# A hybrid layer on one core: group 0 of the mixer taken out of its loop and mixed with the making of the decay tables, and one PSUM bank with fewer early users

## The reference, cut to what matters

```python
zxbcdt = hidden_states @ in_proj_w.T          # gate, x, B, C and dt
xBC = silu(causal_conv4(xBC) + conv_b)
dt = softplus(dt + dt_bias);  A = -exp(A_log) # 128 heads
A_cumsum = cumsum(A * dt)                     # per head, over the tokens
Y_diag = (C B^T * exp(segment_sum)) @ (x*dt)  # inside a chunk
states = ...                                  # from chunk to chunk, decayed
y = (Y_diag + Y_off + D*x) * silu(gate)
out = rmsnorm_per_group(y) @ out_proj_w.T     # 8 groups of 16 heads
```

## Time and profile before

| | us |
|---|---|
| median of 3 runs | 2069.37 (2069.25 to 2069.98) |
| the profiled execution | 2066.19 |
| its span | 2064.4 |
| PE busy | 1975.3 (96%) |
| DVE busy | 1497.6 (73%) |
| ACT busy | 1182.6 (57%) |
| POOL busy | 1033.3 (50%) |
| start of c0 in groups 0, 1 and 2 | 63.27, 263.56, 461.31 |

### The profile page before, as it was taken

How to read it: one execution, slowest core, us unless ns; L and a number is a source line. 1 busy time by engine, 2 the same in 40 slices (tenths; PEclk the granted TensorE clock), 3 DMA queues, 4 the chain that set the end, 5 groups by cost and what they waited for, 6 DMA issues and landing times.

```text
span 2064.4 us, 39384 instructions
## 1 busy us (share of the span) xinstructions
PE 1975.3 (96%) x11776; PEld 1637.7 (79%) x11776; DVE 1497.6 (73%) x2825; ACT 1182.6 (57%) x2569; POOL 1033.3 (50%) x907
## 2 busy tenths in 40 slices
PE   3899999999999999999999999999999999998998
PEld 2688878888888888888888887888788777776876
DVE  6698589859985997699669867985898571186215
ACT  3596369637953784387449645963696325432441
POOL 1288139714960595179318922881497125240433
PEclk7899999999999999999999999999999999999999
DMA  2443035203521451235134313430352049931995
GB/s 86 136 142 103 27 105 163 78 31 116 167 67 38 125 158 51 70 109 145 42 89 124 111 42 94 147 99 27 105 166 75 23 163 387 362 111 42 364 397 182
DMA packets 143909, 261.75 MB, mean 127 GB/s; under 512 B 19536, under 2 KB 35920, under 8 KB 143696
## 3 DMA queue, kind: packets, MB, share of 16 engines
q1 hardware_dynamic: 134848, 231.35, 35.3%
q0 software_dynamic: 7520, 24.65, 3.6%
q10 hardware_dynamic: 1328, 3.15, 0.4%
HBM read 233.38 MB, written 25.69 MB: 125 GB/s over the span
## 4 chain that ended last, share of the span: by engine, by line
PE 65%; issue 20%; DVE 6%; POOL 6%; ACT 1%; DMA 1%; another core or an unknown queue 0%; DVEq 0%; POOLq 0%; SPq 0%; ACTq 0%
PE bank L1602 35%; PE bank L1737 6%; PE bank L1751 5%; PE bank L1892 5%; POOL Y L728 4%; PE bank L1692 4%; PE bank L1904 3%; PE bank L1720 2%; DVE Y L1244 1%; PE bank L1879 1%; PE bank L1711 1%; PE bank L1610 1%; DVE quad L1167 1%; DVE Y L1253 1%; DVE X L1488 1%
## 5 line engine op out<-in xcount | busy, mean ns | idle before, releaser
L1602 PE MATMUL bank<-xh,wh 128*128 128x512 f32 x1288 | 524.3, 407 | 17.1 <-POOL wl L711 13.1
L1602 PE MATMUL bank<-xh,wl 128*128 128x512 f32 x1288 | 505.5, 392 | 0.0
L1602 PE MATMUL bank<-xl,wh 128*128 128x512 f32 x1288 | 502.9, 390 | 0.0
L711 POOL TENSOR_TENSOR wl<-raw,wh 128x512 fp32r<-128x512 f32 x144 | 192.3, 1340 | 486.8 <-ACT wh L886 486.8
L1244 DVE SCALAR_TENSOR_TENSOR Y<-bank,cpar,Y 128x511 f32<-128x511 f32 (+2 forms) x384 | 286.9, 747 | 22.9 <-ACT Y L932 13.8
L1602 PEld LDWEIGHTS bank<-xh,wh 128*128 128x128 f32 x1288 | 243.4, 189 | 65.2 <-issue 18.0
L1602 PEld LDWEIGHTS bank<-xh,wl 128*128 128x128 f32 x1288 | 242.5, 188 | 54.6
L1602 PEld LDWEIGHTS bank<-xl,wh 128*128 128x128 f32 x1288 | 243.8, 189 | 46.1 <-issue 0.5
L728 POOL TENSOR_TENSOR Y<-Y,gt 128x512 f32<-128x512 f32 x128 | 185.8, 1451 | 94.4 <-DVE gt L1298 92.7
L1306 DVE TENSOR_TENSOR al<-Y,ah 128x512 fp32r<-128x512 f32 x128 | 95.7, 747 | 169.1 <-ACT ah L990 169.1
L1602 PE MATMUL bank<-wh,ah 128*128 128x512 f32 x544 | 213.7, 393 | 2.4 <-DVE X L1514 1.7
(11 more groups left out here) (229 smaller groups left out, 4066.0 us busy)
## 6 DMA issues: line engine op xcount, KB each, us to landing
mem<-c_rows SPq DMA_DIRECT2D x128, 256.0 KB, 3.8
mem<-wffn_d SPq DMA_DIRECT2D x62, 512.0 KB
E<-e_rows SPq DMA_DIRECT2D x256, 96.0 KB, 3.3
raw<-wconv_d SPq DMA_DIRECT2D x80, 256.0 KB, 2.7
cv<-c_rows SPq DMA_DIRECT2D x64, 256.0 KB, 3.9
spare<-c_rows SPq DMA_DIRECT2D x64, 256.0 KB, 4.3
raw<-wgate_d SPq DMA_DIRECT2D x64, 256.0 KB, 2.7
raw<-wout_d SPq DMA_DIRECT2D x64, 256.0 KB, 2.7
```

The costliest lines, as they stand in the source:

```text
L711: inc(pool.tensor_tensor(wl[:, W_SLOT[p], :], raw[:, R_SLOT[p], :], wh[:, W_SLOT[p], :], ALU.subtract), w_lo)
L1602: got = mm(out, l, r, start=first and n == 0, stop=last and n == 2)
```

## The change: what it does

1. **Group 0 leaves the loop.** The body of the loop becomes a function `tick(i, k)` on each engine. `tick(0, k)` is written out for all k, then `Fori(1, GROUPS)` runs the rest. The barrier `PH_PREP` is gone.
2. **Preparation is mixed in.** PE does c0, c1 and c2 right after the dt projection, and then the transposes and last-sum products. ACT starts tick 0 after the exponentials of v, makes the row tables after tick 0 and the head tables after tick 3. DVE does its whole polynomial and scan first, then tick 0, the sum table, ticks 1 and 2, the subtraction, tick 3 and so on.
3. **The polynomial is halved.** v, |v|, exp and all polynomial steps run per batch of 512 tokens instead of over 1024. PREP's event numbers grow from 13 to 24 for dt, and so on.
4. **Buffers move** so that the tables and the first tiles don't overlap: tables into the upper half of `Y`, sums into `cv`, dt into `gt`, dt weights into `quad` and slot 10 of `wh`/`wl`. SP no longer waits before the first weights. In group 0 SP asks for the head tables at tick 5 instead of 2, and all row loads come behind that.
5. **Banks.** In groups 1 to 7 the early list is one shorter, and the state bank has one early user. In group 0 all big tiles rotate over banks 0, 1, 2, since the special ones hold preparation data.

```diff
-        EARLY = [ST, OF, DG, 1, 2, 0, ST, OF, DG]
-        BANKS = EARLY + [(k - 2) % 3 for k in range(len(EARLY), NBIG)]
+        EARLY = [ST, OF, DG, 1, 2, 0, OF, DG]
+        LATER = [(k - 2) % 3 for k in range(NBIG)]
+        BANKS = EARLY + LATER[len(EARLY):]
+        def big_bank(i, k):
+            return (LATER if isinstance(i, int) else BANKS)[k]
...
@@ SP
-            sp.wait_ge(dve_self, 1)
-            with sp.Fori(0, GROUPS) as i:
+            group(0, 5)
+            with sp.Fori(1, GROUPS) as i:
+                group(i, 2)
...
@@ ACT
+            for b in range(BATCH):
+                bs = slice(b * SEQ, (b + 1) * SEQ)
+                act.wait_ge(pe_step, b + 1)
+                n = step(nc.scalar.activation(v_hm[:, bs], bank[(DG, ST)[b]][:, :], ACT.Identity, bias=dtb[:, 0:1]))
+                act.wait_ge(act_step, n)
+                n = step(nc.scalar.activation(u_hm[:, bs], v_hm[:, bs], ACT.Abs))
+                act.wait_ge(act_step, n)
+                step(nc.scalar.activation(u_hm[:, bs], u_hm[:, bs], ACT.Exp, scale=-1.0))
...
+            for k in range(NBIG + 4):
+                tick(0, k)
+                if k == 0:
+                    tables_to_rows()
+                if k == 3:
+                    tables_to_heads()
...
@@ DVE
+            for b in range(BATCH):
+                bs = slice(b * SEQ, (b + 1) * SEQ)
+                dve.wait_ge(act_step, 3 * b + 5)
+                step(TS(p_hm[:, bs], u_hm[:, bs], LOG1P[-1], None, ALU.mult))
+                for coefficient in reversed(LOG1P[:-1]):
+                    step(STT(p_hm[:, bs], p_hm[:, bs], coefficient, u_hm[:, bs], ALU.add, ALU.mult))
+                step(STT(dt_hm[:, bs], v_hm[:, bs], 0.0, p_hm[:, bs], ALU.max, ALU.add))
...
+            for k in range(NBIG + 4):
+                tick(0, k)
+                if k == 0:
+                    table_of_sums()
+                if k == 2:
+                    table_of_rests()
...
@@ PE, in tick(i, k), state product u == 0
-                            now(pe, conv_ok, i, len(EARLY))
+                        now(pe, conv_ok, i, 1)
@@ PE, in tick(i, k), diagonal product u == 0
+                        now(pe, conv_ok, i, len(EARLY))
...
+            for k in range(NBIG):
+                tick(0, k)
+                if k == 2:
+                    pe.wait_ge(act_step, 8)
+                    to_tokens(dt_hm, (OF, TR[1]), PREP["dt"])
+                    to_tokens(c_hm, (DG, ST), PREP["scan"])
+                    last_sums()
+            with pe.Fori(1, GROUPS) as i:
```

More of the change, by code:

```diff
@@ L366, in big_bank_free @@
                 return
-            same = [q for q in range(NBIG) if BANKS[q] == BANKS[k]]
+            same = [q for q in range(NBIG) if banks[q] == banks[k]]
             q, wait = (max(q for q in same if q < k), now) if min(same) < k else (max(same), before)
@@ L520, in _ @@
                 for k in range(NBIG + 4):
[L521 to L530, removed]
+                    if k == tables_at:
                         sp.wait_ge(scr_heads, 16)
+                        sp.wait_ge(scr_rows, 32)
                         before(sp, s_ok, i, UNITS)
@@ L844, in _, with tick @@
             step(nc.scalar.activation(acol[:, 0:1], alog[:, :], ACT.Exp))
[L846 to L875, removed]
-            with act.Fori(0, GROUPS) as i:
+            def tick(i, k):
                 def weight_hi(p):
@@ new lines, in tick @@
+                kc = k - 1
+                if 0 <= kc < NCONV:
+                    tile, b = conv_unit(kc)
+                    src = piece(tile, b)
+                    now(act, taps, i, 3 * kc + 3)
+                    inc(nc.scalar.activation(bank[big_bank(i, kc)][:, :], src, ACT.Tanh, scale=0.5), conv_th)
+                u = k - A_
+                if 0 <= u < UNITS:
+                    pair, b = unit(u)
+                    for h in range(2):
+                        n = 2 * u + h
+                        if n == 0:
+                            act.wait_ge(hp_in, 16 * (i + 1))
+                        row_arrived(act, i, n)
+                        for c in range(CH):
+                            last = nc.scalar.activation(
+                                L[n % LR][:, c * P:(c + 1) * P], L[n % LR][:, c * P:(c + 1) * P], ACT.Relu,
+                                scale=-1.0, bias=hp[:, b * CH + c, 0, 2 * pair + h:2 * pair + h + 1])
+                        inc(last, fall_ok)
@@ new lines, in tick @@
+                if NCONV <= k < NCONV + NGATE:
+                    n = k - NCONV
+                    now(act, big_mm, i, k + 1)
+                    if n >= 2:
+                        now(act, y_gated, i, n - 1)
+                    else:
+                        before(act, y_gated, i, NGATE)
+                    inc(nc.scalar.activation(gt[:, n % 2, :], bank[big_bank(i, k)][:, :], ACT.Tanh,
+                                             scale=0.5), gate_th)
+                if k == W_TICK[PIECES - 1]:
+                    weight_hi(PIECES - 1)
@@ new lines, in tick @@
+                for t, m in y_evac(k):
+                    rows_gated(act, i, t, m)
+                    wait, q = (now, t - 1) if t else (before, TT - 1)
+                    if m:
+                        wait(act, big_mm, i, NCONV + NGATE + q + 1)
+                    else:
+                        wait(act, out_half, i, q + 1)
+                    inc(nc.scalar.activation(ah[:, m, :, :], rows_of(t, m), ACT.Copy), y_hi)
+                if k == NORM_AT:
+                    now(act, ss_mm, i, 1)
+                    inc(nc.scalar.activation(sd8[:, :], bank[TR[0]][:, 0:TT], ACT.Sqrt, scale=1.0 / GW,
+                                             bias=eps_c[:, 1:2]), nrm_sd)
@@ new lines, in tables_to_rows @@
+            def tables_to_rows():
+                act.wait_ge(pe_step, 3)
+                for m in range(2):
+                    step(nc.scalar.activation(table(1, m), heads_bank((OF, TR[1])[m]), ACT.Copy, scale=0.5))
+                act.wait_ge(dve_self, PREP["scan"])
+                act.dma_start(c_rows.rearrange("g h n -> (g h) n"), c_hm).then_inc(scr_rows, 16)
+                n = step(nc.scalar.activation(v_hm, c_hm, ACT.Exp))
+                act.wait_ge(act_step, n)
+                act.dma_start(e_rows.rearrange("g h n -> (g h) n"), v_hm).then_inc(scr_rows, 16)
@@ new lines, in tables_to_heads @@
+            def tables_to_heads():
+                act.wait_ge(dve_self, PREP["diff"])
+                n = step(nc.scalar.activation(table(2), table(2), ACT.Exp))
+                assert n == PREP["decay"], n
+                for m in range(2):
+                    n = step(nc.scalar.activation(table(3, m), heads_bank((OF, DG)[m]), ACT.Exp))
+                assert n == PREP["cend"], n
+                act.wait_ge(act_step, n)
+                act.dma_start(heads_scratch[:, :, 0:HPW].rearrange("g p n -> p g n"),
+                              tables_rows.rearrange("p (g n) -> p g n", g=GROUPS)).then_inc(scr_heads, 16)
```

818 lines of the change are left out of this document (395 added, 423 removed).

## The result

| kernel, same chip | median us | lowest to highest | profiled execution | its span |
|---|---|---|---|---|
| before | 2069.68 | 2069.25 to 2070.47 (4 runs) | 2066.19 | 2064.4 |
| after | 2036.78 | 2035.59 to 2039.36 (4 runs) | 2037.09 | 2035.0 |

The change takes 32.9 us off the median, where 26.0 were forecast, so the measured time lies just under the low end of the range (2037.0). The two profiled executions differ by less, 29.1 us, and their spans by 29.4. The other 3.8 us are the choice of executions: the profiled one of before lies 3.5 us under its own median, that of after 0.3 us above its own.

What follows compares the result with a forecast made beforehand. PE, busy 96% of the span, was taken as the bound, so only its waits or low clock could yield time. Group 0's 19.2 and the banks' 6.8 sum to 26.0 us: 2069.37 to 2043.4 us, range 2037 to 2054.

Steps and rivals of the forecast that it cites:

- these two places: PE's hole while decay tables are made (28.60 to 63.27 us), and its 8 waits for DVE's L1253, 9.9 us.
- The bank edit: Groups 1 to 7: state product starts 1.24 us earlier; PE gains 0.97 us a group, 6.8 us in all.
- the wait only moves: Rival: c11 or the diagonal products hold PE instead, groups 1 to 7 give 0: 2050.2 us, 12%.
- Group 0: Preparation and first tiles overlap, c11 starts at 82.9 instead of 102.16; gain 19.2 us, bounds 12 and 24.
- The polynomial's term: Group 0, DVE: 22 half-width steps of 0.70 us, 15.4 us; dt ready at 43.3, scans end at 46.5.
- the slack of 0.47 us: Before the third diagonal product, between DVE's L1269 releasing it and PE beginning it; added to group 0's 18.7 us.
- That bound (up to 3 us): Group 0's start: layer norm up to 3 us later if the queue is shared between x and first weights.
- The waits of c3 to c10: Group 0 on three banks: one wait of about 1 us in each second tile.
- the rival with a low clock: Rival: low clock from c3 to c10, group 0 gains about nothing; 2064.6 at the slow end, 9%.
- the slower one: Rival: low clock lasts beyond c10 into group 0's unit ticks; ten such ticks give about 2095 us, 3%.
- The rival with fewer stalls in group 0: Warm sums and DVE always fed: up to 24 us gained in group 0, 2038.6 us, 10%.
- The median's offset: The median lies 3.2 us above the profiled execution, so the forecast starts from 2069.37, not 2066.19.

Runs made afterwards that it cites:

- x2: Kernel before with only group 0 written out ahead of the loop; barrier, banks and order of work kept: 2052.73 us, 0.9970 of before.
- x4: Changed kernel with a one-column tanh on ACT between group 0 and the loop: 2033.85 us, 0.9886 of before.
- x1: Kernel before with the bank edit alone, in all 8 groups: 2052.70 us against 2059.70 for before, 0.9966.
- x3: Kernel before, loop untouched, with a one-column square root on ACT right ahead of the loop: 2055.09 us, 0.9982 of before.
- x0: Changed kernel again, unchanged, as reference on another chip: 2028.52 us against 2060.36 for before, 0.9839.
- x0b: Changed kernel once more, unchanged, on a further chip: 2039.33 us against 2071.17 for before, 0.9854.
- x5: Changed kernel with the polynomial's halving taken back, 1024 columns as before: 2031.02 us, 0.9857 of before.
- x6b: Repeat of x6 on the chip of x0b: 2037.53 us, 0.9845 of before.
- x6: Changed kernel with the first two weight pieces copied by ACT, and so split by POOL, ahead of the exponentials: 2026.59 us, 0.9838 of before.
- x7: x6 with ACT's head-table work in two parts, after ticks 3 and 4: 2038.25 us, 0.9842 of before.

## Why the prediction was right or wrong, step by step

**The step that failed** is the sentence "All else in the mixer is PE's own work, so these two places are what the change can reach". In PE's waits there was a third place in the mixer, L1602 waiting 7 times for POOL's L711, 5.1 us in total. I took it for something that the change leaves as it is, and gave no reason. x2 to x4 show what it was: a table load at the head of the loop, there because the preparation's exp and not sqrt precedes the loop, and gone as soon as a group is written out ahead of it. In the marks it is worth 0.78 us a group, 7 x 0.78 = 5.5 us, entered in the sum as 0. The period showed it: about 196.8 us was forecast for it, and 195.93 came. With the load in the sum the prediction would have been near 2038.

**The bank edit** was right in mechanism and size: 0.90 us a group in x1 against 0.97, 6.3 us for seven groups. The wait did reappear ahead of c11, as argued: in group 1, DVE's SiLU (L1238) released c11 at 279.11, and PE began it at 279.15. The rival "the wait only moves" holds in this much, but the period shows that most of it came through. c11 of group 1 lies 35.21 us behind c0 in x1 (263.21 to 298.42) and 35.08 in after (244.07 to 279.15), where 35.2 to 35.6 were to show that the step is right. PE's chain of waits there:

```profile
278.42 0.69 DVE Y L1238
279.11 0.04 issue
279.15 3.02 PE bank L1624 x12
282.17 0.67 PE bank L1690 x6
282.84 0.44 PE bank L1718 x4
283.28 1.06 PE bank L1736 x16
```

**Group 0** was forecast at 19.2 us and gave 18.5. Of that 0.9 may not be the change's: the dt projection began at 20.55 instead of 21.42, since DVE waited less for x. It began at 20.3 to 20.9 in all eight traces of changed kernels, and at 21.65, 20.57 and 21.41 in x1, x2 and x3, which issue the weights as before, so this stays open. Without it group 0 gave 17.6. Step by step:

| step | forecast | measured |
|---|---|---|
| c0 starts | 32.6 | 31.87 |
| c2 ends | 43.3 | 43.0 |
| dt ready | 43.3 | 44.7 |
| scan ends | 46.5 | 48.0 |
| last sums end, c3 starts | 53.9 | 54.94 |
| c3 ends | 57.4 | 57.8 |
| head tables issued | 61.1 | 61.24 |
| `conv_ok` 9 | 82.8 | 83.4 |
| c11 starts | 82.9 | 83.62 |

The polynomial's term is the one off, by 1.4 us: the nine steps of the first half took 8.44 us and not 6.50, beside POOL's split. The 0.70 us a step came from rows of steps that read one operand from PSUM, where the 6.50 of the undisturbed half are 0.72 a step. That is 1.94 us, and DVE's earlier start (27.33 for 27.9) took 0.6 of it back. c3 began 1.0 us late, ended 0.4 late, since it ran at full clock from its start where I had 1.6 us of low clock, and c11 began 0.7 late. That c3 gave this back is luck of the one execution: it took 2.85 us here, 3.11 in x0, 2.95 in x0b and 3.95 in x5. Of the slack of 0.47 us 0.3 came in: DVE's state copy is at 83.93, 18.2 us earlier than in the earlier trace rows, and PE kept 18.5.

x itself was not delayed by the 1 MB of weights behind it. That bound (up to 3 us) was not needed.

**The waits of c3 to c10** were forecast at about 1 us in each second tile. PE waited only three times in the eight tiles, 0.73 us before c5, 0.31 before c6 and 0.26 before c10. DVE waited 0.25 to 0.80 us for ACT's first taps of c4 to c8, under the 1 us a tile that was to count against the step. The granted clock from 54.90 to 83.60 was 1.00, so the rival with a low clock fell, and with it the slower one. From 59 to 85 us it was 1.00 in the seven other traces of changed kernels too; below 1.00 in some of them was only c3, right behind the last sums at 0.50. The Trainium skill's rule that the prediction weighed ("TensorE: Matmul & The Clock Gate", section "A second HAM failure mode: psum-queue depth-cycling") had little here to act on: three such waits did not lower the clock, and what waits in every second tile would do no run shows.

**The rival with fewer stalls in group 0** (2038.6) had the number nearest to the measured 2036.8, for a wrong reason: group 0 did not gain 24 us but 18.5. The additional microseconds came from groups 1 to 7. Only the mark in each group tells the two apart.

**The median's offset.** I carried over that the median lies 3.2 us above the profiled execution. In the kernel after it lay 0.3 us below it. That is 3.5 of the 6.6 us by which the forecast was off, and it is chance of which execution was profiled, not a term of the change. The other 3.1 are the difference between the two profiled executions, 29.1 against 26.0. Of the span it is 29.4, so 3.4 more than forecast: table load +5.5, group 0 -0.7, banks -0.5, between the marks and not assigned +0.7, work behind the mixer -1.6.

## What to carry to other kernels

Read each row of the bottleneck's waits, the ones that recur once in each pass of a loop above all, and ask what the releaser itself did in the 3 us before. A wait at the head of a loop may be there only because of the state in which the loop is entered; x3 took it away with a one-column operation ahead of the loop. And price a step on DVE by rows in which POOL was as busy as it will be in the new place.

## What the runs showed of the hardware

- A table load took 1.283 us each time, and where the compiler puts it depends on what ran before the loop: exp or tanh, at the head of each pass (before, x1, x4); sqrt, at the first tanh of the pass (after, x2, x3).
- At each loop edge ACT had 2.0 to 2.3 us in which it waited for nothing the profile shows, with or without a load (before, x3 and after). Where group 0 was written out and the loop followed, there was none: ACT's copy at 239.43 stood right behind the operation from 238.89. Without a load behind it, PE waits at most 0.3 us at the head of a group (x3).
- Nine dependent DVE steps of 128x512 with both inputs in SBUF took 6.50 us alone and 8.44 to 8.46 beside one POOL split of two pieces, which itself took 2.95 instead of 2.51. The three taps of 128x511 with one input in PSUM took 2.31 beside a split too (after: taps at 54.52, a split of one piece at 55.27).
- The granted clock at one and the same place differed between executions of nearly the same work. The dt projection ran at full clock throughout in x5 and x6b and began at half of it in after. c3, behind 3.5 to 3.8 us of last sums at 0.50 to 0.54, took 2.85 us at a mean of 1.00 in after and 3.95 at 0.70 in x5.
- From the last mark to the end of the span the same instructions took 451.4 and 453.0 us on the first chip, 443.7 to 447.8 in x1 to x4, 442.3 to 444.1 in x0, x5 and x6, and 456.0 to 459.2 in x0b, x6b and x7. The mixer's last mark of the changed kernel repeats within 1.5 us in its three traces (1582.0, 1583.4, 1583.5), while the spans are 2035.0, 2027.5 and 2039.5. So the 12 us between x0 and x0b, on two chips, arise behind the mixer. Why was not settled.
